# A three-stage decoder kernel: projections by quad of heads, rotary embedding read out of PSUM, output projection summed early, new order lists

## The reference

```python
x = layernorm(x + attn(x))          # stage a
x = layernorm(x + mlstm(x, ctx))    # stage b
x = layernorm(x + ffn(x))           # stage c
```

## Time and profile before

| | us |
|---|---|
| median of 3 runs (2749.26 to 2753.19) | 2750.72 |
| the profiled execution | 2750.88 |
| its span, first to last instruction | 2749.2 |
| TensorE busy | 2388.7 |
| VectorE busy | 1873.4 |
| ScalarE busy | 1592.4 |
| GpSimd busy | 850.4 |

### The profile page before, as it was taken

One profiled execution on the slowest core, in us unless ns is written; L12 is line 12 of the kernel. 1 busy time (PEld: TensorE's weight loads), 2 busy tenths in 40 slices (PEclk: granted clock), 3 DMA queues, 4 the chain that ended last, 5 costly groups with the idle time before them and its releaser, 6 DMA issues.

```text
span 2749.2 us, 52882 instructions
## 1 busy us (share of the span) xinstructions
PE 2388.7 (87%) x19200; PEld 1932.4 (70%) x19200; DVE 1873.4 (68%) x4590; ACT 1592.4 (58%) x4810; POOL 850.4 (31%) x1065
## 2 busy tenths in 40 slices
PE   4778999888899888898988889998889898888974
PEld 3566777767777777777776777777777777677763
DVE  3457767777767677776776776767676777777653
ACT  3346675556665555666556666555566655666732
POOL 1122333332333332333333233333233333323321
PEclk9789999999999999999999999999999999999976
DMA  3010111111111111011111011111101111101111
GB/s 106 8 39 24 31 46 41 47 47 33 31 40 39 47 47 45 23 35 40 47 47 47 26 30 47 39 47 47 47 18 38 39 47 47 47 24 32 39 31 39
DMA packets 267318, 109.76 MB, mean 40 GB/s; under 512 B 215218, under 2 KB 248114, under 8 KB 267058
## 3 DMA queue, kind: packets, MB, share of 16 engines
q1 hardware_dynamic: 258354, 89.61, 13.3%
q10 hardware_dynamic: 8704, 16.78, 1.6%
HBM read 89.57 MB, written 16.78 MB: 39 GB/s over the span
## 4 chain that ended last, share of the span: by engine, by line
PE 64%; DVE 20%; ACT 11%; issue 4%; SPq 1%; DMA 1%; ACTq 0%; POOL 0%; DVEq 0%; POOLq 0%
PE ps_g L572 48%; PE ps_g L580 10%; PE ps_s L572 5%; DVE neg_max L1203 2%; DVE pt_all L1445 2%; DVE ctx_t L1348 2%; ACT decay L905 2%; DVE x_bo L1485 1%; DVE ln_stat_a L1163 1%; DVE ln_stat_c L1163 1%; DVE ctx_t L1346 1%; DVE ln_stat_b L1163 1%; DVE x_res L1253 1%; ACT ctx_t L905 1%; DVE p_t L1230 1%
## 5 line engine op out<-in xcount | busy, mean ns | idle before, releaser
L905 ACT ACTIVATE p_a<-ps_s,neg_max 128x128 f32<-128x128 f32 (+1 forms) x1024 | 415.6, 436 | 26.8 <-DVE neg_max L1203 26.8
L1535 POOL TENSOR_TENSOR p_t<-p_t,const 128x512 f32<-128x512 f32 x128 | 239.5, 1871 | 415.2 <-DVE p_a L1184 410.0
L572 PE MATMUL ps_g<-x_t_hi,wqkv_hi 128*128 128x256 f32 x1024 | 294.5, 288 | 17.0 <-DVE x_t_lo L1176 16.7
L580 PE MATMUL ps_g<-const,p_a 128*128 128x128 f32 x1536 | 248.0, 285 | 48.4 <-DVE x_t_lo L1450 20.3
L572 PE MATMUL ps_g<-x_t_lo,wqkv_hi 128*128 128x256 f32 x1024 | 287.5, 281 | 0.0
L572 PE MATMUL ps_g<-x_t_hi,wqkv_lo 128*128 128x256 f32 x1024 | 287.5, 281 | 0.0
L1203 DVE TENSOR_REDUCE neg_max<-ps_s 128x2 f32<-128x256 f32 (+1 forms) x512 | 256.6, 547 | 16.7 <-PE ps_s L572 16.7
L905 ACT ACTIVATE y_out<-x_bo,ln_shift_c,ln_rstd_c 128x512 f32<-128x512 f32 x64 | 48.7, 807 | 352.4 <-DVE ln_shift_c L1495 352.4
L1620 POOL TENSOR_SCALAR p_all<-p_all,f_rec,g_bc 128x256 f32<-128x256 f32 x256 | 139.0, 554 | 335.9 <-DVE f_rec L1436 335.9
L926 ACT COPY p_t<-ps_g 128x512 f32<-128x512 f32 x128 | 75.1, 586 | 286.0 <-PE ps_g L572 286.0
L580 PEld LDWEIGHTS ps_g<-const,p_a 128*128 128x128 f32 x1536 | 171.7, 143 | 98.0 <-DVE x_t_lo L1450 27.4
(11 more groups left out here) (206 smaller groups left out, 6956.8 us busy)
## 6 DMA issues: line engine op xcount, KB each, us to landing
x_tok<-in_x SPq DMA_DIRECT2D x32, 512.0 KB, 3.7
ctx<-in_ctx SPq DMA_DIRECT2D x64, 256.0 KB, 3.4
p_all<-in_L_ffn_Wq SPq DMA_DIRECT2D x128, 128.0 KB, 2.5
pt_all<-in_L_ffn_Wk SPq DMA_DIRECT2D x128, 128.0 KB, 3.0
y_out<-in_L_ffn_Wv SPq DMA_DIRECT2D x128, 128.0 KB, 3.1
out<-y_out ACTq DMA_DIRECT2D x32, 512.0 KB, 2.8
x<-in_L_attn_Wqkv SPq DMA_DIRECT2D x2, 512.0 KB, 8.0
const<-tables SPq DMA_DIRECT2D x1, 518.0 KB
```

What stands on the lines that cost most here:

```text
L572: return nc.tensor.matmul(o, l, r, start=first, stop=last)
L580: return nc.tensor.transpose(o, i, ident)
L905: return nc.scalar.activation(o, i, f, **kw)
L1535: g.tensor_tensor(raw, raw, c["cos"].unsqueeze(1).to_broadcast([P, 2, T]), ALU.mult).then_inc(cos_scaled.sem)
```

## The change

- **Quads.** `qk` bank u now holds q and k of quad u (heads 4u to 4u + 3). TensorE's order is bank 0, values 0, scores(0), values 1, bank 1; banks 2 and 3 come between the turns and `att` of quad 0. `scores(u)` waits for `roped` u + 1.
- **Rotary out of PSUM.** ScalarE's copy is gone. VectorE shuffles the bank into one `qk_rot` (each quad waits for the add of the one before), multiplies the bank by cos into `qk` and so frees it, GpSimd multiplies `qk_rot` by sin, VectorE adds.
- **Output projection.** The sums over quads 0 to 2 (9 matmuls for each half of the tokens) are issued ahead of and behind `att` of quad 3; only 3 each stand behind its `att_lo`.
- **m_col** comes ahead of decay; m_row lies in the decay buffer.
- The mask is loaded once into p_t instead of the table; the 128 columns of ones become one, broadcast.
- All five strings of `ORDER`, and `BANKS`, are new. Among what they do, read out of them: TensorE begins with ctx t = 0, x t = 0, ctx t = 1, x2 t = 0, x1 t = 0, x t = 1, x1 t = 1, x2 t = 1, then bank 0, gate_t, logit. wo, y's statistics and x2 stand ahead of the last output matmuls. On VectorE r_lg stands behind the rotary add of quad 0. On ScalarE the cast of the q weights stands ahead of the exponentials of pairs 0 and 1, the casts of the k and v weights behind them, then the copy of values 1, then decay; the bank of values 1 (`"v": "12"`) is that of the first decay (`"decay": "20"`).

```diff
 TensorE, stage a
-            for u in range(QUADS):
+            def rotary(u):
                 o = bank[("qk", u), b]
...
-                        n = (2 * u + m) * P
+                        n = (m * QUADS + u) * P
...
+            def projected(t, first, last):
+                for k in range(first, last):
+                    done = mm3(bank[("out", t), b], part(att_t, slice(None), k, slice(t * P, (t + 1) * P)), part(wout_s, slice(None), k), k == 0, k == KT - 1)
+                return done
+
             def scores(u):
-                pe.wait_ge(*roped(b, 3 + u // 2))
+                pe.wait_ge(*roped(b, u + 1))
...
+            yield from rotary(0)
+            yield from values(0)
             scores(0)
             for _ in range(5):
                 yield
+            yield from values(1)
+            yield from rotary(1)
...
+                if u == QUADS - 1:
+                    pe.wait_ge(*att_lo(b, QUADS - 1))
+                    pe.wait_ge(*freed[("out", 0), b])
+                    projected(0, 0, KT - 1)
...
+                if u == 0:
+                    yield from rotary(2)
+                    yield from rotary(3)
...
+                if u == QUADS - 1:
+                    pe.wait_ge(*freed[("out", 1), b])
+                    projected(1, 0, KT - 1)
...
+            pe.wait_ge(*att_lo(b))
+            for t in range(TT):
+                projected(t, KT - 1, KT).then_inc(filled.sem)
 VectorE, stage a
+            def rotary(u):
+                raw = bank[("qk", u), b]
+                yield
+                yield
+                if b or u:
+                    dve.wait_ge(*(roped(b, u) if u else roped(b - 1)))
+                dve.wait_ge(*full[("qk", u), b])
+                v.stream_shuffle(qk_rot.rearrange("p m n -> p (m n)"), raw, [(i + DA // 2) % DA for i in range(DA)]).then_inc(shuffled.sem)
                 if b:
                     dve.wait_ge(*scored(b - 1))
-                v.tensor_tensor(qk[:, 2 * u:2 * u + 2, :], raw, rot, ALU.add).then_inc(roped.sem)
+                v.tensor_tensor(qk[:, 2 * u:2 * u + 2, :], raw.rearrange("p (m n) -> p m n", m=2), c["cos"].unsqueeze(1).to_broadcast([P, 2, T]), ALU.mult).then_inc(dve_emptied.sem)
+                yield
+                dve.wait_ge(*empty[("qk", u), b])
+                dve.wait_ge(*sin_scaled(b, u + 1))
+                v.tensor_tensor(qk[:, 2 * u:2 * u + 2, :], qk[:, 2 * u:2 * u + 2, :], qk_rot, ALU.add).then_inc(roped.sem)
+                yield
 GpSimd, stage a
                 pool.wait_ge(*shuffled(b, u + 1))
-                g.tensor_tensor(raw, raw, c["cos"].unsqueeze(1).to_broadcast([P, 2, T]), ALU.mult).then_inc(cos_scaled.sem)
+                g.tensor_tensor(qk_rot, qk_rot, c["sin"].unsqueeze(1).to_broadcast([P, 2, T]), ALU.mult).then_inc(sin_scaled.sem)
 TensorE, stage b
-            mm(o[:, HX:2 * HX], ones, log_f[:, 0, :], True, False)
+            mm(o[:, HX:2 * HX], c["one"].to_broadcast([P, P]), log_f[:, 0, :], True, False)
```

More of the change, by code:

```diff
@@ L57 @@
+        "ababbaac"
     ),
@@ L748, in stage_b @@
                 yield
-            o = bank[("m_col",), b]
-            pe.wait_ge(*freed[("m_col",), b])
-            for t in range(TT):
-                done = tr(o[:, t * HX:(t + 1) * HX], m_row[:, t * P:(t + 1) * P], eye[0:HX, 0:HX])
-            done.then_inc(filled.sem)
-            yield
-            yield
             for h in range(HX):
@@ L918, in stage_a, with values @@
                 yield
-            for u in range(QUADS):
-                yield
-                yield
-                act.wait_ge(*full[("qk", u), b])
-                if u > 1:
-                    act.wait_ge(*roped(b, u - 1))
-                nc.scalar.copy(qk_raw[u % 2].rearrange("p m n -> p (m n)"), bank[("qk", u), b]).then_inc(act_emptied.sem)
-                yield
-                yield
-            for t in range(TT):
+            def values(t):
                 yield
@@ L951, in exps @@
                 e.then_inc(exped.sem)
+            for _ in range(4):
+                yield
+            yield from values(0)
             for _ in range(3):
@@ L980, in stage_a @@
                     yield
+                if u == 0:
+                    for _ in range(2 * 4):
+                        yield
                 yield
@@ L1209, in stage_a @@
             maxes(1)
-            yield
-            yield
-            yield
+            for _ in range(3 + 3):
+                yield
+            yield from rotary(1)
             for u in range(QUADS):
@@ L1235, in stage_a @@
                         yield
-                for _ in range(5):
+                for _ in range(3):
                     yield
+                if u == 0:
+                    yield from rotary(2)
+                    yield from rotary(3)
+                yield
+                yield
                 dve.wait_ge(*r_spread(b, u + 1))
@@ L1304, in stage_b @@
             yield
+            yield
+            dve.wait_ge(*full[("m_col",), b])
+            v.tensor_tensor(m_col, bank[("m_col",), b][:, 0:TT * HX].rearrange("p (t h) -> p t h", t=TT), cum_f, ALU.add).then_inc(dve_emptied.sem)
+            yield
             for hp in range(HX // 2):
@@ L1529, in stage_a, with rotary @@
                 yield
-            for u in range(QUADS):
-                raw = qk_raw[u % 2]
+            def rotary(u):
+                yield
                 yield
```

147 lines of the change are left out of this document (65 added, 82 removed), and 8 rows, old and new, of the table BANKS.

## The result

The changed kernel takes 2791.7 us (median of four executions, 2784.4 to 2798.3), beside 2750.0 for the kernel before (2747.2 to 2753.2): a ratio of 1.0151, 95% interval 1.0134 to 1.0168. It is slower by about 42 us. The forecast was 2721, and the time lies above the end of the range, 2788.

A forecast was written before the change was run, and what follows sets the result against it. TensorE, busy 87%, was taken as the bound, with the weights' chain through ScalarE's casts deciding the first decay matmul. Steps of 80.9 against 81.4 us save 15, filling 15: 2750.9 - 15 - 15 = 2721 us, range 2672 to 2788.

The forecast's parts named there:

- Head: From T, the end of the output projection's last matmul, to the projections: they start at T + 7.6 instead of 11.85.
- GpSimd's multiply: Quad 0's rotary multiply on GpSimd: 1.27 us instead of 1.78, with 1.8 kept as the upper bound.
- r_lg at 13.2: VectorE's router step behind quad 0's rotary add: at T + 13.2, with the add taken as 0.6 us.
- Indices to the q weights, 6.55 us: From the expert indices at 15.1 to the q weights in SBUF at 21.6, read in the last step.
- The wait at g: TensorE's wait at g, ahead of the first decay matmul: under 1 us.
- Casts, exponentials, copy, 8.15 us: ScalarE from the q weights at 21.6 through casts, table load, eight exponentials and value copy, ending at 29.8.
- The rest, 50.6: From the first decay matmul to the step's end: 48.7 us of work plus 1.9 of waits.
- The low clock, 0.4: TensorE's 1.2 GHz costs about 2 us of quad 0 in one step in five, 0.4 on the mean.
- Filling: First two steps: earlier scores and output projection sums save 15 us together, bounds 5 and 22.
- Draining: The two last steps, bound by stage c: unchanged.
- The slower one: Weights' chain costs more than the head gives: multiply stays 1.8, clock low into quad 0; 2780 us, chance 0.25.
- The faster rival: Low clock vanishes from the head, waits after T + 30 are hidden; step 79.2, 2670 us, chance 0.18.

The follow-up runs named there:

- x2bo_late: Changed kernel with GpSimd's addition of x2 and the bias moved behind the product of the gathered bias: 2751.3 us.
- filler: Changed kernel plus twenty matmuls a step with unread results, ahead of TensorE's wait for the first decay matmul's bank: 2758.8 us.
- the router's kernels: Changed kernel with the router ahead of quad 0's rotary on three engines: 2622.2 us; with GpSimd's addition of x2 and the bias also late, 2605.4 us.
- copy_first: Changed kernel with ScalarE's copy of value tile 1 moved ahead of the casts of the k and v weights: 2701.0 us.
- router_first: Changed kernel with only orders changed, the router ahead of quad 0's rotary on TensorE, ScalarE and VectorE: 2622.2 us.
- x2bo_first: Changed kernel with GpSimd's addition of x2 and the bias moved ahead of quad 0's rotary multiply: 2840.8 us.
- late_sums: Changed kernel with the early output projection sums undone, both tiles summed whole behind att_lo: 2971.2 us.

## Why the prediction was wrong, step by step

**Head: right.** TensorE was at 1.2 GHz for 4.8 us of the mean head in the kernel before and is not in this one. Forecast projections at T + 7.6, measured 7.36; quad 0's end forecast at 10.5, 10.36 in the step shown.

**GpSimd's multiply: right.** 1.28 us, mean 1284 ns over 128, where the earlier trace rows had 1.78 beside VectorE's own multiply and 1.27 alone.

**r_lg at 13.2: wrong, 14.37.** This is the step of the prediction that failed first. It named r_lg's queue ("behind the rotary add of quad 0, which waits for GpSimd's multiply") and priced the add at 0.6. It asked what runs beside the multiply and not what GpSimd does next. The lists say it: x2_bo's addition is next, and starts with the multiply's end, as the add does. 0.69 became 1.71. (The add is 1.0 of the 1.17; the other 0.15 is still there in x2bo_late, 13.35 against 13.2.) Beside that row stands the rule I had cited for the multiply: the Trainium skill, SBUF — State Buffer, section Who interferes with whom, has a VectorE instruction with two SBUF inputs contend with a GpSimd instruction that reads SBUF. The add has two SBUF inputs, and GpSimd reads. The trace agrees with the rule in both places, 1.28 instead of 1.78 and 1.71 instead of 0.69; I had weighed it for one instruction only. x2bo_late shows its worth: 40 us.

**Indices to the q weights, 6.55 us: too small.** 7.0 in the step shown (1424.10 to 1431.11), and 0.7 more than forecast between r_lg and the q cast in the mean, with 22.7 to 25.2 for that cast in steps whose r_lg differs by 0.4. The row I took was that of the last step. The trace narrows it: the four loads of the q weights are issued by 4.6 us behind the indices in the step shown and by 4.4 in that last step, so the time is in their landing, the last of which comes 6.5 to 9.0 us behind the indices. What makes the landing slower and less even in full steps was not tried. The wait at g, forecast under 1 us, was 1.3 on the mean (42.1 in 32); with the add unstretched in x2bo_late it fell to 11.3 in all.

**Casts, exponentials, copy, 8.15 us: right** (1431.11 to 1439.17 are 8.06).

So the decay matmul is at 31.69: 29.9 + 1.17 + 0.7, less 0.1. **The rest, 50.6: as work 0.6 too long.** It is 50.0 in filler and in the router's kernels and 50.4 in copy_first, all with the full clock. **The low clock, 0.4: wrong.** I took the clock to fall in one step in five, in the head. It never fell there. It fell behind the new wait in 22 of 29 steps, where I had forecast a TensorE that stands idle and then priced the idle time alone. filler gives its cost, 1.64 us in the mean step, where the forecast had 0.4 altogether. By luck the 0.6 of work too much hid half of that: measured, the rest is 51.65 against the forecast 51.0. (In 8 steps the clock fell at about T + 18 as well or instead; the decay matmul, which waits for ScalarE, came only 0.1 us later in them.)

The sum: 83.33 against 80.9 is 2.43 a step: 1.17 at r_lg, 0.7 the weights, 1.24 the clock less 0.6 of work, less 0.1. Times 29 this is 70 us, and the time missed the forecast by 71. Counted whole, the 30 full steps missed by 76, the filling gave back 6.6, and draining took 2.0.

**Filling: too small,** 21.6 us in the two filling steps against 15. Step 0 gave 10.3, as forecast (68.85 was to become about 59); step 1 gave 11.3, where the forecast had half of step 0's. Draining lost 2.0 where nothing was forecast.

**The rivals.** The slower one, 2780 at 0.25, was the case. It said that the decay matmul would start at 31.9 and the step take 82.9, and that this decides once the chain is over 1 us late; measured 31.69 and 83.33. Its place and its price came out by luck, for neither of its reasons held: the multiply didn't stay at 1.8, and the clock was not low in quad 0. It had 0.5 + 1.5 from them; the add and the weights happened to bring 1.17 + 0.7. The faster rival had said "ScalarE's chain of casts has no way around" against itself. copy_first and router_first are two ways around, by nothing but the order. The chances were the second mistake: the text noted five queues in a row with no slack, and gave the case that any of them slips 0.25. Where five links stand in a row without slack, each surprise in any of them is paid, and there were two (the add and the weights).

## What to carry to other kernels

When an edit puts an operation on a chain without slack, look up in the lists what both engines do during it and right behind it; a stretched neighbour is not seen in the busy shares. A wait of TensorE of some 2 us costs more than its length when the clock falls behind it (here 1.64 us on top of 1.8), so a forecast idle piece needs a term for the clock. And where several transfers hang on an index, compute that index first: moving sixteen numbers ahead of a rotary embedding brought 170 us here.

## What the runs showed of the hardware

VectorE's normalization with one SBUF tensor and two scalar columns was stretched as well, from 1.00 to 2.88 us for two of 512 columns (x2bo_first), beside a GpSimd addition that had started 0.07 us ahead; GpSimd's two took 2.66 then. I had taken only operations with two SBUF inputs for endangered, and left out the exception when I cited the rule. The Trainium skill, SBUF — State Buffer, section Who interferes with whom, counts `tensor_scalar` among the operations that can enter a mode with both ports and then block or are blocked for the whole instruction; the trace agrees, 1.88 us for two.

TensorE fell to 1.2 GHz after 2.0 us in which it did nothing, and stayed there for 6.7 us though it was fully busy; in late_sums a wait of 1.4 us was followed by 6.5 us at 1.2 GHz, with a second wait inside them. Twenty matmuls a step whose result nobody reads, put into the wait, kept the clock at 2.4 GHz behind it and shortened the kernel by 33 us.
